# A new order for the first part of the experts' stage, with the norms' roots split between GpSimd and VectorE

## What is computed

```python
h = _layernorm(x, axis=-1) * (1 + cb) + sb
x = x + gb * _L1_ffn_ref(h, ...)
# _L1_ffn_ref:
logits = jnp.einsum('th,eh->te', x, gate_w)
scores = jax.nn.softmax(logits, axis=-1)
topk_w, topk_idx = lax.top_k(scores, 2)          # 2 of 8 experts, weights normalised to 1
def body(acc, ew):
    w1e, w2e, cwe = ew
    g, u = jnp.split(x @ w1e, 2, axis=-1)
    return (acc + cwe[:, None] * (jax.nn.silu(g) * u @ w2e), None)
moe, _ = lax.scan(body, jnp.zeros_like(x), (w1, w2, cw.T))
shared = (silu(x @ sw1.T) * (x @ sw2.T)) @ sw3.T
return moe + shared
```

## Time and profile before

| | us |
|---|---|
| median of 3 runs | 1194.93 (1194.69 to 1197.26) |
| the profiled execution | 1193.11 |
| its span | 1191.2 |
| busy in the span: PE, DVE, ACT, POOL | 1073.6, 916.4, 735.7, 343.3 |
| mean granted TensorE clock, share of full | 0.948 |

### The profile page before, as it was taken

How to read it: one execution, slowest core, us unless ns; L and a number is a source line. 1 busy time by engine, 2 the same in 40 slices (tenths; PEclk the granted TensorE clock), 3 DMA queues, 4 the chain that set the end, 5 groups by cost and what they waited for, 6 DMA issues and landing times. The chain is left out here.

```text
span 1191.2 us, 21657 instructions
## 1 busy us (share of the span) xinstructions
PE 1073.6 (90%) x7276; PEld 919.8 (77%) x7276; DVE 916.4 (77%) x1850; ACT 735.7 (62%) x1389; POOL 343.3 (29%) x353
## 2 busy tenths in 40 slices
PE   5879787768999999999999999999999987769995
PEld 4645555546889899989998999899989976659993
DVE  6688889847778778778788788788787776787775
ACT  5668686756666566666665666666666653635650
POOL 3376454453311101110111111101111333863440
PEclk8789798979999999999999999999999996899998
DMA  7210000119304003003003003012000001444426
GB/s 276 68 45 10 15 6 15 41 43 90 86 3 123 10 10 116 9 9 116 9 9 116 9 10 115 9 38 86 9 18 27 1 1 42 131 151 117 125 91 220
DMA packets 62325, 72.16 MB, mean 61 GB/s; under 512 B 21841, under 2 KB 49617, under 8 KB 61234
## 3 DMA queue, kind: packets, MB, share of 16 engines
q1 hardware_dynamic: 58850, 61.90, 19.3%
q0 software_dynamic: 3408, 9.39, 2.1%
HBM read 36.39 MB, written 32.78 MB: 58 GB/s over the span
## 5 line engine op out<-in xcount | busy, mean ns | idle before, releaser
L1447 PE MATMUL attn_psum<-all_h_parts,attn_wp 128*128 128x512 f32 x1152 | 300.7, 396 | 0.0
L1447 PEld LDWEIGHTS attn_psum<-all_h_parts,attn_wp 128*128 128x128 f32 x1152 | 211.1, 188 | 40.8
L1602 ACT CAST attn_pp<-attn_p 128x512 fp32r<-128x512 f32 (+3 forms) x256 | 117.3, 458 | 199.4 <-DVE attn_p L1696 197.3
L1827 POOL TENSOR_TENSOR all_gate<-all_gate,attn_sq 128x512 f32<-128x512 f32 x64 | 84.6, 1321 | 502.1 <-ACT attn_sq L1613 502.0
L1677 DVE TENSOR_TENSOR attn_pp<-attn_p,attn_pp 128x512 fp32r<-128x512 f32 (+3 forms) x256 | 198.8, 777 | 8.1 <-ACT attn_pp L1602 8.1
L1526 PE MATMUL attn_psum<-attn_qkp 128*128 128x512 f32 (+3 forms) x768 | 164.4, 323 | 4.5 <-DVE attn_qkp L1677 4.5
L1473 PE MATMUL attn_psum<-attn_pp,attn_vp 128*128 128x512 f32 (+3 forms) x768 | 162.9, 321 | 0.8 <-issue 0.4
L1473 PEld LDWEIGHTS attn_psum<-attn_pp,attn_vp 128*128 128x128 f32 x768 | 129.0, 189 | 21.2 <-issue 1.3
L1526 PEld LDWEIGHTS attn_psum<-attn_qkp 128*128 128x128 f32 x768 | 125.1, 189 | 13.1 <-DVE attn_qkp L1677 3.0
L1696 DVE TENSOR_TENSOR attn_p<-attn_psum,attn_mask 128x512 f32<-128x512 f32 (+3 forms) x256 | 123.8, 484 | 4.9 <-PE attn_psum L1526 3.7
L983 DVE TENSOR_REDUCE front_top<-front_psum 128x2 f32<-128x256 f32 (+3 forms) x128 | 100.9, 816 | 25.8 <-PE front_psum L644 25.7
(11 more groups left out here) (368 smaller groups left out, 1834.4 us busy)
## 6 DMA issues: line engine op xcount, KB each, us to landing
expert_rows<-attn_empty SPq DMA_DIRECT2D x8, 2080.0 KB, 10.3
all_wraw<-in_w1p SPq DMA_DIRECT2D x8, 1024.0 KB, 5.1
all_yacc<-expert_rows SPq DMA_DIRECT2D x39, 130.5 KB, 2.2
attn_mask<-decay_masks SPq DMA_DIRECT2D x16, 256.0 KB, 2.6
experts_wx<-expert_results SPq DMA_DIRECT2D x6, 512.0 KB, 8.6
experts_xraw<-in_wx SPq DMA_DIRECT2D x4, 608.0 KB, 4.1
all_wraw<-in_wx SPq DMA_DIRECT2D x4, 608.0 KB, 4.0
all_x<-in_x SPq DMA_DIRECT2D x4, 512.0 KB, 7.4
```

The costliest lines, as they stand in the source:

```text
L1447: last = nc.tensor.matmul(out, wp[:, a, k, col:col + P], hh[:, c, k, b * S:(b + 1) * S], start=(m == 0), stop=(m == 5))
L1602: nc.scalar.copy(pp[:, u % 2, 0, cols], p[:, cols]).then_inc(p_hi, 1)
L1827: nc.gpsimd.tensor_tensor(cols, cols, sq[:, h, :], ALU.add).then_inc(summed, 1)
```

## The change

It does four things. (1) `pool_rstd` is split: epsilon and negation move to DVE, right behind `stats(b)`; the power stays on POOL as `pool_power`; the product becomes `norm_shift(b)` on DVE. (2) On POOL, `pool_power(2)` stands ahead of `scatter(0, 0)`, `pool_power(3)` between `scatter(0, 1)` and `scatter(1, 0)`. (3) The lists of PE, ACT and DVE for the first part are written anew: DVE does `w_lower(0)`, `gate_y(2)` and `add_y(2)` ahead of `choose(0)`, and `stats(2)` ahead of `meta(0)` and `slots(0)`; the last split of weights, `w_lower(7)`, stands ahead of `choose(3)`. (4) In the tail batch 2 goes the way of the first three pieces (three DVE operations), and only batch 3 goes through PE, half by half.

```diff
+    def vector_eps(self, nc, dve, b):
+        dve.wait_ge(self.aggr_done, b - 1)
+        nc.vector.tensor_scalar(self.rstd[:, b], self.mv[:, b, :, 1], EPS_LN, None, ALU.add).then_inc(self.var_eps, 1)
+        nc.vector.tensor_scalar(self.shift[:, b], self.mv[:, b, :, 0], -1.0, None, ALU.mult).then_inc(self.negated, 1)
+
+    def pool_power(self, nc, pool, b):
+        pool.wait_ge(self.var_eps, b - 1)
         nc.gpsimd.tensor_tensor(self.rstd[:, b], self.rstd[:, b], self.t["neg_half"][:, 0:TB], ALU.pow
                                 ).then_inc(self.rstd_done, 1)
+    def vector_shift(self, nc, dve, b):
+        dve.wait_ge(self.negated, b - 1)
+        dve.wait_ge(self.rstd_done, b - 1)
+        nc.vector.tensor_tensor(self.shift[:, b], self.shift[:, b], self.rstd[:, b], ALU.mult).then_inc(self.shift_done, 1)
...
                 norm.pool_rms(nc, pool)
+                norm.pool_power(nc, pool, 2)
                 scatter(0, 0)
-                norm.pool_rstd(nc, pool, 2)
                 scatter(0, 1)
-                norm.pool_rstd(nc, pool, 3)
+                norm.pool_power(nc, pool, 3)
                 scatter(1, 0)
```

And the tail:

```diff
-                for b in (2, B - 1):
-                    pe.wait_ge(results_in[b + 1], 32)
-                    for half in range(2):
...
+                pe.wait_ge(results_in[B], 32)
+                for half in range(2):
+                    for c in range(2):
+                        tt = (B - 1) * TB + 2 * half
+                        last = nc.tensor.matmul(bank(Y_BANK + half), t["ident"][:, :],
+                                                results[:, c, tt:tt + 2, :].rearrange("p t n -> p (t n)"),
+                                                start=False, stop=(c == 1))
                     last.then_inc(pair_made, 1)
...
-                for i, part in enumerate(PARTS[:3]):
+                for i, part in enumerate(PARTS[:4]):
...
+                for half in range(2):
+                    dve.wait_ge(pair_made, half + 1)
+                    nc.vector.tensor_tensor(upd[:, 2 * half:2 * half + 2, :],
+                                            ps[:, Y_BANK + half, :].rearrange("p (t n) -> p t n", t=2),
+                                            t["gate"][:, 3, B - 1:B, :].to_broadcast([P, 2, D]), ALU.mult).then_inc(y_gated, 1)
+                    dve.wait_ge(y_gated, 5 + half)
+                    nc.vector.tensor_tensor(x[:, part, :], x[:, part, :], upd[:, 2 * half:2 * half + 2, :], ALU.add
+                                            ).then_inc(x_final, 1)
```

More of the change, by code:

```diff
@@ L2405, in _ @@
                 turn_logits(3)
-                gates(3)
+                down(1)
                 token_rows(3, 1)
                 rank(3)
-                ups(3)
                 gates(4)
                 route.tensor_count(nc, pe, bank(ROUTE_BANK))
+                ups(4)
                 down(2)
-                ups(4)
                 down(3)
@@ L2689, in stats, with norm_shift @@
                     norm.vector_stats(nc, dve, b)
+                    norm.vector_eps(nc, dve, b)
+                def norm_shift(b):
+                    norm.vector_shift(nc, dve, b)
                 def norm_low(b):
@@ L2701, in _ @@
                 norm.vector_means(nc, dve, bank(R_BANK))
+                w_lower(0)
+                gate_y(2)
+                add_y(2)
                 choose(0)
-                gate_y(2)
+                stats(2)
                 meta(0)
                 slots(0)
-                add_y(2)
                 norm_low(1)
-                stats(2)
+                norm_shift(2)
+                w_lower(1)
                 gate_y(3)
-                hide(0)
                 add_y(3)
```

152 lines of the change are left out of this document (62 added, 90 removed).

## The result

The changed kernel takes 1191.8 us in the median of its executions, the kernel before 1197.63 in the same comparison: a ratio of 0.9949 (95% interval 0.9935 to 0.9962). The forecast was a gain of 4.3 us, a ratio of 0.9964 on the 1194.93 us of the front. One of the 20 executions of the changed kernel took 2041.88 us and is left out of the ratio; why it did is not known.

The account below looks back on a forecast made before the run. POOL's stream of 32 indirect writes was taken to bound the experts' first part, DVE next. First part -4.0, tiles 0, tail -0.3 gave -4.3 us: 1194.93 to 1190.6, range 1187.6 to 1195.0.

Parts of the forecast that it names:

- The first write: POOL's first indirect write in the experts' stage: waits for slots(0), starts at 1013.0, 2.5 us later than before.
- The roots: pool_rstd of batches 2 and 3 on POOL: 7.5 us go, 2.4 us stay for batch 3's held power.
- POOL never starves: POOL's writes of batches 1 to 3 never wait for DVE's places: slack 2.9 us, then 4 to 5.
- The holds: POOL's writes from write 9 on, stretched by two-input DVE operations: about 4.5 us, against 4.9 before.
- DVE's slack: DVE's third output product ends at about 1062.3, with 5.5 us of slack to PE's first tile at 1067.8.
- rival 2: First part: DVE becomes the bound or POOL starves once, norm_shift(3) parking DVE; 5 to 9 us more, 1194.5; chance 0.08.
- The tiles: PE's tiles after the first part: same work, zero change, with 1 us to either side.
- The tail: End of kernel: PE does only batch 3's 8 records, in 5.6 us; gain 0.3 us, bounds -1.1 and +0.9.
- 1: POOL's stream starts later or is held more: gain only 0.3 to 2.4 us, say 1193.5; chance 0.20.
- 3: TensorE's clock stays at 1.2 GHz much longer in the first part: slower, 1199; chance 0.07.
- 4: POOL's writes hold some 20 two-input DVE operations about 0.5 us each, 10 us: 1195.1; chance 0.03.
- 5: More than forecast: fewer holds, an early first write, no issue delay; gain 6.5 us, 1188.4; chance 0.09.

Follow-up runs that it names:

- before_again: The kernel before, unchanged, profiled and compared with itself again; ratio to before 1.0028 (1.0008 to 1.0048).
- rows_high: The changed kernel with the low part of the split left out of token_rows for batches 1 to 3, 4 matmuls instead of 8; ratio to before 0.9966.
- thin_loads: The changed kernel loading only 8 of 1216 columns of the weights of experts 2 to 7; ratio to before 0.9979.
- roots_whole: The changed kernel with pool_rstd whole on POOL again, in the places of the two powers; ratio to before 0.9960.
- rank_late: The changed kernel with rank(1) moved behind token_rows(1, 1) and ups(0) on PE; ratio to before 0.9978.
- gates_late: The changed kernel with gates(2) moved from in front of rank(1) to right behind it on PE; ratio to before 0.9932.
- ranks_first: The changed kernel with gates(2) behind token_rows(1, 1) and rank(2) ahead of token_rows(2, 1) on PE; ratio to before 0.9930.
- before_dense: The kernel before with eight unread transposes of the identity added on PE between norm_turn(2) and gates(2); ratio to before 1.0006.
- head_only: The changed kernel with the tail of the kernel before; ratio to before 0.9975.
- tail_only: The kernel before with only the new tail; lists, POOL's order and pool_rstd as before; ratio to before 0.9986.
- one_input: The changed kernel with w_lower of experts 3 to 7 reading one input, the raw weight times zero; ratio to before 0.9967.

## Why the prediction was right, step by step

**The forecast** was -4.3 us; the two comparisons gave -6.1 and -4.3 us (by their ratios), and the stage is 2.8 us shorter than in before's profile and 5.5 shorter than in before_again's. It came out right in total while several of its terms were off and partly made up for each other; that it lies between the 2.8 us of the profiles and the 6.1 of the first comparison is in part luck.

**The first write** was put 2.5 us later than before; it is 1.2 later (at 15.2, forecast 16.4). DVE's walk was right within 0.3 us: the places of batch 0 are known at 14.9 after the stage's start, forecast 15.1. The term that failed is the 1.2 us of issue, taken from how the write followed ACT: it starts at 1016.44, 0.3 us after the end of `slots(0)` at 1016.13.

**The roots.** POOL's second power stood in the sum with 2.4 us, as held by `w_lower(2)`; it took 1.05 us and was not held, the other end that I kept (1.3 with its issue). That was worth nothing, because *POOL never starves*, the step with 2.9 us of slack, is the one that failed. The power ended at 1028.58, and with the 0.57 of issue of the earlier trace rows write 9 could have started at 1029.1, at 27.9. It started at 30.7 since `meta(1)` ended at 1031.2, and `meta(1)` was late by DVE's 3.0 us before `slots(1)`, which no row of before could show. That write 9 stands within 0.4 us of the forecast 30.3 is two errors that cancel: a stream 2.5 us faster than forecast (1.3 from the first write, the rest from a power that was not held) and a wait of 2.9.

**The holds** of writes 9 to 32 were forecast at 4.5 us and 0.4 for the map, and measured 4.9 (27.9 us busy, less 24 x 0.96). But for the gaps of 0.78 and 1.61 us before writes 17 and 25 (0.48 and 1.31 over the usual 0.30), the end of the stream would have been the forecast one: 67.4 less 1.8, less the 0.4 at write 9, is 65.2, against 65.4 forecast. So of the first part's -4.0, the stream gave -2.05 (69.46 to 67.41) and the tile -1.7 (75.23 to 73.55).

**DVE's slack** of 5.5 us is used up: its third product ends at 72.2, forecast 65.7. The two waits for PE's late signals are 5.9 of these 6.4 us. The slack had also been read off the wrong tile. PE waits for the third product ahead of the first tile, and the 1071.80 of the earlier trace rows is the second. The first tile, in before and in after:

```profile
1070.75 0.66 PE L2430 MATMUL experts_psum<-all_ident,all_yacc 128*128 128x128 f32 x2 [5.14 <-DMA all_yacc<-expert_rows]
```

```profile
1073.92 0.41 PE L2433 MATMUL experts_psum<-all_ident,all_yacc 128*128 128x128 f32 x2 [1.73 <-DMA all_yacc<-expert_rows]
```

Before, it is turned 3.9 us after the third product's end, not 4.9. After, it is turned 0.47 us after it (1073.45), and in every profile with the new lists but that of rows_high (1.66) this distance is 0.46 to 0.49. So in the new order DVE's third product bounds the first tile, level with its load, and the second tile waited 0.50 us for its own load. Where it waited for none (thin_loads) it was turned 0.25 us behind the first; so POOL's stream alone could have brought no more than about 0.7 us. This is rival 2 by half. Its sign (a gap before writes 9, 17 and 25) is there and DVE did become a bound, but its price of 5 to 9 us came as 2.9 at write 9 and 5.9 on DVE, most of it covered, and its reason, `norm_shift(3)` parking DVE, is not what happened: the waits are at `slots(1)` and `slots(2)`.

**The tiles** took 89.9 us from the tile of the table to the last write of results, before 90.3: zero, with the bound of 1.

**The tail** was put at -0.3 with bounds of -1.1 and +0.9 of gain; it gave -0.8. The 8 records took 6.47 us, forecast 5.6, since the clock did not rise until the last of them (over the ten profiles with the new tail 5.2 to 6.7); that term was 0.9 too small. Against it, PE could start 15.4 us after the first load of results was issued, and I had read 16.7 from the DMA share. The last half on DVE was 1.4, as forecast.

**The rivals.** 1: the first write was early and the holds as forecast; false. 3: the granted clock stood at 0.50 for some 16 us of the first part in all, the last of it to 1048, and for some 27 in before, counted to the tile; false. 4: no `w_lower` in after took more than 1.42 us, and those that began inside a running write took 1.41 to 1.43 in both profiles, as the earlier trace rows had shown; false. The 0.05 us under before_again falls where the two start within 5 to 17 ns, and why wasn't tested. 5: by the profile false, with 2.85 us of gain, though the -6.1 us of the first comparison comes near its 6.5.

## What is shown and what stays open

Shown: the new order, not the split of the roots, carries the first part's gain (roots_whole); in the new order PE's signals come 2.8 to 5.7 us after the recorded ends at `rank(1)`, in every profile of it; this doesn't come from the weights' loads (thin_loads) nor from `rank` itself (rank_late); with less work of PE in front it shrinks by 1.5 us (rows_high, gates_late, ranks_first). With `rank(1)` moved forward the tile came 2.6 and 2.4 us sooner, in one profile each of two kernels; in rows_high the same lateness less brought 0.2.

Open: what holds PE's signals up. That it is the amount of work in front was contradicted by before_dense, where more of it did nothing at that place. There is no late signal in before and before_again, one of 9.0 us in before_dense, and of changing length for `hide` and `down` in the same lists (head_only against after). Nor is it bound to the new order: tail_only has the lists of before, and there the signal of `rank(2)` came 1.3 us late and DVE waited 2.6 us for it, 1.3 in before. I have no rule that tells in advance where it strikes. The 2.9 us left of it in gates_late were not taken away by anything tried. The indirect writes of the rows as a cause were not taken away.

One rival touches all of it: that the recording itself holds PE up. All lateness was seen in profiled executions, for in others there is nothing to see it by. The traces of before and before_again, the two without a late signal, hold 9490 and 9484 records of raised semaphores; the other twelve hold 8295 to 8416, and most of the missing ones are of DMA landings in the experts' stage. Records are missing where signals are late, and no run tells which comes of which, or whether unprofiled executions have late signals at all. That the comparisons gave 4.3 and 6.1 us and the two profiles only 2.8 would fit with it, but the stages ahead, which vary by 6.8 us over the profiles, can make such a difference as well.

## What to carry to other kernels

Where an order by hand puts a small matmul whose result another engine waits for behind large ones, don't take the recorded end of the small one for the time of its signal: look at the first instruction that waits for it, and put the small one in front (here the tile came about 2.5 us sooner for one moved line, in a profile). Two signals that come together though their matmuls end apart say that the work was done and the signal was held up. A step costed at nothing by a slack of 3 us needs a slack on the signal as well as on the work. Read a slack to the instruction that really waits, here the first tile and not the second. And before a gain of 0.3% is believed, run the unchanged kernel against itself.

## What I had not expected of the hardware

- Signals of PE 2.8 to 5.7 us after the recorded end of the matmul at `rank(1)`, once 9.0 (before_dense), in stretches where every waiting engine sees the delay, and with several signals let out within 0.17 us (after: 27.51 to 27.68).
- A hold is decided by a few ns and is worth 1.27 us: the same write of the same program took 0.96 us when it started 17 ns after DVE's operation (before) and 2.23 us when it started 22 ns after (before_again).
- A `tensor_scalar` with one input in SBUF, 0.78 us for 1216 columns where the two-input operation takes 1.42, held POOL's indirect DMA in the same way, until 0.82 us after its end, in the one case that one_input has.
